# Two routed sublayers of a decoder: how scatters, sums and the hand-over to the next block are ordered

## Time and profile before

| | us |
|---|---|
| median of 3 runs | 3512.28 (3511.22 to 3514.16) |
| the profiled execution: its time | 3504.94 |
| the profiled execution: its span | 3503.2 |
| busy in the span: PE, DVE, ACT, POOL | 2806.8, 2181.1, 1821.2, 1838.3 |
| `moe_first`: to the last eviction | 463.5 |
| `moe_last`: from its first expert output to the end | 3230.1 to 3503.2 |

### The profile page before, as it was taken

The page is one execution under the profiler, slowest core; times in us unless marked ns, Lnnn a source line. Parts: engine busy times, 40 slices in busy tenths (PEclk is TensorE's granted clock), DMA queues, the critical chain, the costliest instruction groups (busy, mean ns, idle before and its releaser), DMA issues. The chain is left out here.

```text
span 3503.2 us, 84294 instructions
## 1 busy us (share of the span) xinstructions
PE 2806.8 (80%) x28622; PEld 1994.2 (57%) x28638; DVE 2181.1 (62%) x5986; ACT 1821.2 (52%) x3448; POOL 1838.3 (52%) x1742
## 2 busy tenths in 40 slices
PE   2799877978888699826469998996888679996984
PEld 2788855745555466514336665664444446665873
DVE  3022346568887588751458876776999767884124
ACT  0444447445555466502136666774567766662441
POOL 4642655347766555444655546663133755553436
PEclk9999988999999799955579999997999989996997
DMA  9565520200110221117411112221000012213653
GB/s 339 148 189 160 162 83 25 8 23 35 42 43 37 69 72 67 61 54 193 118 39 53 57 55 90 91 90 39 1 1 1 5 37 62 76 66 111 172 156 109
DMA packets 327245, 283.50 MB, mean 81 GB/s; under 512 B 111382, under 2 KB 244921, under 8 KB 326588
## 3 DMA queue, kind: packets, MB, share of 16 engines
q1 hardware_dynamic: 285324, 230.00, 22.1%
q0 software_dynamic: 16384, 33.59, 3.2%
q10 hardware_dynamic: 25264, 16.40, 1.5%
HBM read 135.30 MB, written 60.69 MB: 56 GB/s over the span
## 5 line engine op out<-in xcount | busy, mean ns | idle before, releaser
L939 DVE TENSOR_TENSOR moe_first_tile_y<-moe_first_out_ps,moe_first_expert_w 128x256 f32<-128x256 f32 x85 | 35.9, 422 | 272.1 <-PE moe_first_out_ps L1084 271.8
L797 POOL DMA_INDIRECT moe_first_token_y<-slot_y,moe_first_slots x128 | 125.0, 976 | 98.2 <-DMA slot_y<-moe_first_tile_y 59.5
L1895 POOL TENSOR_TENSOR causal_k_blocks<-causal_k_T,headmask 128x1024 f32<-128x1024 f32 x64 | 121.4, 1899 | 99.6 <-PE causal_scores L1505 94.0
L1895 POOL TENSOR_TENSOR alibi_k_blocks<-alibi_k_T,headmask 128x1024 f32<-128x1024 f32 x64 | 121.3, 1898 | 94.0 <-PE alibi_scores L1505 90.0
L1084 PEld LDWEIGHTS moe_first_out_ps<-moe_first_expert_down,moe_first_hid 128*128 128x128 f32 x1360 | 167.5, 194 | 5.4 <-issue 0.6
L1162 POOL DMA_INDIRECT slot_x<-x_tok,moe_first_slots x128 | 124.8, 975 | 85.8 <-issue 36.7
L1084 PE MATMUL moe_first_out_ps<-moe_first_expert_down,moe_first_hid 128*128 x1360 | 167.4, 277 | 0.4 <-issue 0.4
L1895 POOL TENSOR_TENSOR full_k_blocks<-full_k_T,headmask 128x1024 f32<-128x1024 f32 x64 | 120.8, 1898 | 84.9 <-PE full_scores L1505 79.9
L3188 PE MATMUL L_ffn_experts<-weights_odd,x_T 128*128 128x512 f32 x256 | 141.8, 637 | 12.3 <-ACT L_ffn_expert_out L3288 11.2
L1895 POOL TENSOR_TENSOR keys_k_blocks<-keys_k_T,headmask 128x1024 f32<-128x1024 f32 x64 | 120.9, 1900 | 45.6 <-PE keys_scores L1505 42.0
L3111 DVE SCALAR_TENSOR_TENSOR L_ffn_combined<-L_ffn_expert_out,L_ffn_mix,L_ffn_combined 128x128 f32<-128x128 f32 x448 | 138.9, 373 | 4.0
(11 more groups left out here) (580 smaller groups left out, 9044.1 us busy)
## 6 DMA issues: line engine op xcount, KB each, us to landing
moe_first_expert_w<-in_L_attn_experts SPq DMA_DIRECT2D x85, 322.0 KB
moe_last_expert_w<-in_L_ffn_experts SPq DMA_DIRECT2D x53, 322.0 KB
moe_first_tile_x<-slot_x SPq DMA_DIRECT2D x85, 128.0 KB, 2.7
slot_y<-moe_first_tile_y SPq DMA_DIRECT2D x85, 128.0 KB
slot_x<-blank ACTq DMA_DIRECT2D x2, 4992.0 KB, 43.0
L_ffn_tile_x<-slot_x SPq DMA_DIRECT2D x32, 256.0 KB, 3.2
slot_y<-L_ffn_tile_y SPq DMA_DIRECT2D x32, 256.0 KB
moe_last_tile_x<-slot_x SPq DMA_DIRECT2D x53, 128.0 KB, 2.4
```

Source lines behind the costliest of these rows:

```text
L797: pool.indirect_dma_start(y_in[:, p, k, r, :], None, slot_y[part][0:NTS[part] * SLOT_TILE, :], bass.IndirectOffsetOnAxis(slots[:, part, r, ...
L939: dve.tensor_tensor(y_out[:, q, :, :], out_bank[j % 2][:, 0:SLOT_TILE].rearrange("p (s d) -> p s d", s=SPAN), over(wall[:, j % RING, FF + ...
L1895: pool.tensor_tensor(k_blocks[:, t.p, :, :], keys.to_broadcast([128, 8, TILE]), lanes.to_broadcast([128, 8, TILE]), ALU.mult).then_inc(spr ...
```

## The change

Scatters of all parts are issued one after another with no wait on evictions, ahead of all gathers. The order on POOL is then: for each chunk, three of the next chunk's four tiles are gathered, then the inverse deviation, then the fourth. SP asks for the weights of tile j+5 ahead of the rows of tile j+8. The sums get new places (`DUE`): 37, 41, 45, 49 and 66, 69, 72, 75, 78, 81 in `moe_first`; 18, 21, 24, 27 and 41, 43, 45, 47, 49 in `moe_last`. What has no place by tile J - 4 is `held`: chunks 10 to 15 in `moe_first`, which the next block gets, and chunks 9 to 15 in `moe_last`, which follow its tile loop. Transposes and stores of a chunk come one tile later. In the block after `moe_first` a handed chunk takes two steps instead of three, with two tiles gathered in each. The gather of chunk 10 stays in `moe_first`.

```diff
--- before.py
+++ after.py
@@ -760,13 +760,14 @@
         def due(c):
 
             part = part_of[c]
-            if part == parts - 1:
-                return None
-            return reach[part + 1] + 3 + chunks[part].index(c) * (NTS[part + 1] - 4) // len(chunks[part])
-
-        after_tile = {due(c): c for c in range(CHUNKS) if due(c) is not None}
-        last_chunks = chunks[-1]
-        late = [] if hand_over else last_chunks
+            settle, apart = DUE[part]
+            return reach[part + 1] + settle + apart * chunks[part].index(c)
+
+        DUE = ((14, 4), (4, 3)) if top == 2 else ((3, 3), (3, 2))
+        FIRST = next(c for c in chunks[1] + [chunks[2][0]] if c in chunks[2] or due(c) > J - 4)
+        held = range(FIRST, CHUNKS)
+        after_tile = {due(c): c for c in range(FIRST)}
+        late = [] if hand_over else held
 
         def combine(dve, c):
             p, part = c % 2, part_of[c]
@@ -1002,13 +1003,13 @@
                 for j in range(8):
                     load_slots(j)
                 for j in range(J):
+                    if j + 5 < J:
+                        load_expert(j + 5)
                     if j + 8 < J:
                         load_slots(j + 8)
-                    if j + 5 < J:
-                        load_expert(j + 5)
                     store_slots(j)
-                    if j - 2 in after_tile:
-                        tail.store(sp, after_tile[j - 2])
+                    if j - 3 in after_tile:
+                        tail.store(sp, after_tile[j - 3])
                 for c in late:
                     tail.store(sp, c)
                 tail.all_stored(sp)
@@ -1099,8 +1100,8 @@
                     if j + 2 < J:
                         hidden(j + 2)
                     output(j)
-                    if j - 2 in after_tile:
-                        tail.transpose(pe, after_tile[j - 2], route_bank)
+                    if j - 3 in after_tile:
+                        tail.transpose(pe, after_tile[j - 3], route_bank)
                 for c in late:
                     tail.transpose(pe, c, route_bank)
 
@@ -1145,84 +1146,71 @@
                         copy_turned(j // 2 + 2)
                     if j + 2 < J:
                         activate(j + 2)
-                    if j - 2 in after_tile:
-                        tail.copy_transposed(act, after_tile[j - 2], route_bank)
+                    if j - 3 in after_tile:
+                        tail.copy_transposed(act, after_tile[j - 3], route_bank)
                 for c in late:
                     tail.copy_transposed(act, c, route_bank)
 
             @block.gpsimd
             def _(pool):
-                def scatter(part, some):
-
-                    pairs = top * sizes[part]
-                    for n in some:
+                def scatter(part):
+                    for n in range(top * sizes[part]):
                         t, r = divmod(n, top)
-                        if part and n % 2 == 0 and n:
-                            pool.wait_ge(out_done, reach[part - 1] + n * (NTS[part - 1] - 6) // pairs)
                         pool.indirect_dma_start(slot_x[part][:, :],
                                                 bass.IndirectOffsetOnAxis(slots[:, part, r, t:t + 1], 0),
                                                 net.x_tok[:, origin[part] + t, :], None).then_inc(scattered[part], 16)
-
-                def finish_chunk(c):
-                    if c == chunks[part_of[c]][0]:
-                        gather(pool, c, range(PER))
-                    if c + 1 < CHUNKS and part_of[c + 1] == part_of[c]:
-                        gather(pool, c + 1, range(PER))
-                    tail.inverse_std(pool, c)
 
                 for part in range(parts):
                     pool.wait_ge(net.cleared[part], 16)
                     net.await_rows(pool, part)
                     pool.wait_ge(planned, 2 * part + 2)
-                    pairs = top * sizes[part]
-                    if part < 2:
-                        scatter(part, range(pairs))
-                        continue
-                    turns = len(chunks[part - 2])
-                    for n, c in enumerate(chunks[part - 2]):
-                        finish_chunk(c)
-                        scatter(part, range(pairs * n // turns, pairs * (n + 1) // turns))
-                for some in chunks[max(parts - 2, 0):]:
-                    for c in some:
-                        if not hand_over or c not in last_chunks:
-                            finish_chunk(c)
+                    scatter(part)
+                gather(pool, 0, range(PER))
+                for c in range(FIRST):
+                    before = PER - 1 if part_of[c] == part_of[c + 1] else 0
+                    gather(pool, c + 1, range(before))
+                    tail.inverse_std(pool, c)
+                    gather(pool, c + 1, range(before, PER))
+                for c in late:
+                    if c + 1 < CHUNKS:
+                        gather(pool, c + 1, range(PER))
+                    tail.inverse_std(pool, c)
 
         if not hand_over:
             return
         ctx.close()
-        FIRST = last_chunks[0]
 
         def late_gpsimd(pool):
             def rows(c):
-                m, third = divmod(c, 3)
-                if m < len(last_chunks):
-                    gather(pool, FIRST + m, ((0, 1), (2,), (3,))[third])
+                m, half = divmod(c, 2)
+                if 1 <= m < len(held):
+                    gather(pool, FIRST + m, ((0, 1), (2, 3))[half])
 
             def inverse_std(c):
-                m, third = divmod(c, 3)
-                if third == 0 and m < len(last_chunks):
+                m, half = divmod(c, 2)
+                if half == 0 and m < len(held):
                     tail.inverse_std(pool, FIRST + m)
 
             return [(-5, rows), (-1, inverse_std)]
 
         def late_vector(dve):
             def weighted_sum(c):
-                m, third = divmod(c, 3)
-                if third == 0 and m < len(last_chunks):
+                m, half = divmod(c, 2)
+                if half == 0 and m < len(held):
                     combine(dve, FIRST + m)
 
             def normalise(c):
-                m, third = divmod(c, 3)
-                if third == 0 and m < len(last_chunks):
+                m, half = divmod(c, 2)
+                if half == 0 and m < len(held):
                     tail.normalise(dve, FIRST + m)
 
             return [(-2, weighted_sum), (0, normalise)]
 
         def late_tensor(pe, bank, host):
             def transpose(c):
-                m, third = divmod(c, 3)
-                if third == 0 and m < len(last_chunks):
-                    if m:
+                m, half = divmod(c, 2)
+                if half == 0 and m < len(held):
+                    if c >= 3:
                         pe.wait_ge(host.xT_copied, c - 2)
                     tail.transpose(pe, FIRST + m, bank)
 
@@ -2007,7 +1995,7 @@
 
     def copied_by(self, step):
 
-        return self.first + min(CHUNKS - self.first, max(0, (step + 2) // 3))
+        return self.first + min(CHUNKS - self.first, max(0, (step + 1) // 2))
 
 
 class Flow:
```

## The result

The changed kernel takes 3465.82 us (median of 4 runs, 3463.55 to 3468.67), the kernel before beside it 3513.22. The ratio is 0.9866, with a 95% interval from 0.9849 to 0.9883: 47 us faster, where 66 were forecast. The profiled execution took 3465.42 us with a span of 3463.7, that is 39.5 us less than the span of the profiled execution before; before's other runs lie 6 to 9 us above its profiled one, which is the difference between 39.5 and 47. The mean clock is 0.896 in both.

A forecast was written before the change was run, and what follows sets the result against it. No engine was busy throughout; PE stalls from paced scatters, and evictions held while DVE waited for gathers or deviations, were taken as the loss. Front -37.7 and end -28.4 gave -66.1: 3438.8 profiled, 3446 expected, range 3436 to 3468.

The forecast's parts named there:

- Part 1, scatters: Routed sublayers: unpaced scatters remove PE's boundary stalls, 16.51 + 1.49 + 3 and 8 us in `moe_first`, 11 and 17.5 in `moe_last`.
- the 1 us of the sum: Start of `moe_first`: price taken for DMA traffic of scatters beside the first rows and weights, bounds nothing to 7 us.
- Part 2, weights ahead of rows: SP's queue at part boundaries: weights no longer stand behind the wait for rows; counted zero, bound 1.5 us.
- Part 3, places of the sums: `moe_first`: sums spaced by the gathers' rate, 3 tiles apart, so tile 84 is evicted at 408.5 instead of 463.1.
- The terms -54.6 and +1: `moe_first`: saving of 54.6 us to the last eviction, and 1 us lost to DMA traffic at the start.
- Part 4, the hand-over: Block after `moe_first`: six handed chunks, two overlapping steps each, rounds of 21 us; 2.3 us less ahead, price 16.8.
- The term of 16.8: Block after `moe_first`: price in us of handing over six chunks, 112.2 to attention chunk 10's moments where before 95.4.
- The rivals of a round of 26.9 or 38 us: Hand-over rounds stay as long as three-step ones (+25 us, 3471, chance 0.10), or steps don't overlap (3536, chance 0.03).
- DVE shutting POOL out: Block after `moe_first`: rival that six handed sums and normalisations each stop POOL, +20 us, 3466, chance 0.04.
- The front's sum, -37.7: First sublayer and the block after it, in us: -54.6 + 1.4 + 1 - 2.3 + 16.8.
- the 2.3 of the rounds: Block after `moe_first`: 12 gathers instead of 14 ahead of the first handed deviation, 16.5 us instead of 18.8.
- Part 5, the end: Last sublayer: without stalls and with closer sums, the last gather starts at 3457.9 instead of 3486.34, saving 28.4 us.

## Why the prediction was right, and which of its steps were not

**Part 1, scatters.** Right on the chips of the kind that the profile before came from, step by step: scatters every 1.265 us to 192.5, no wait of PE at a boundary in either sublayer. The start was 0.6 us later (first eviction 94.91 instead of 94.34), within the 1 us of the sum. That the trace of one chip doesn't show what scatters do to PE elsewhere was not among the rivals. That both stalls went because the pacing did is read from the timelines: no run on such a chip took the pacing alone away or put it back.

**Part 2, weights ahead of rows.** Counted as nothing; no run changes it alone, so this is neither shown nor refuted.

**Part 3, places of the sums.** Last eviction 407.8 against 408.5 and the later start. DVE's waits for the gathers' sums are gone, and what is left is 10 waits for the deviation, 13.4 us together, while PE waits 0.2 us in the whole loop. The terms -54.6 and +1 measured as 407.8 - 463.1 = -55.3.

**Part 4, the hand-over.** Two steps a chunk overlap as argued. The term of 16.8 measured as 114.5 - 95.4 = 19.1: the first round took 23.3, and DVE's next sum stands ahead of the first normalisation there (that this is the cause was not tested). The rivals of a round of 26.9 or 38 us fall. The price of the first was worked out wrongly, too: three rounds of 26.9 instead of 21 cost 17.7 us and not 25. DVE shutting POOL out falls as well: the gathers beside the handed sum at 417.0 took 0.95 to 1.00 us. The 1.16 us of the earlier trace rows is not shown to be DVE's doing: that gather is the first behind other work of POOL, and the one at 326.99, the first behind a wait, took 1.09 with DVE idle.

**The step that was missing: the end of the sublayer.** The forecast lets the block begin 1.6 us after the last eviction, as before, and adds 1.4 for chunk 9's transposes. It began 9.1 after it. POOL now works until the end, and its drain, which had ended together with SP's work, lies open: 9.1 - 3.0 = 6.1 us. The front's sum, -37.7, measured as 548.7 - 580.3 = -31.6 us at attention chunk 10. The 6.1 missing are the drain; the 2.3 of the rounds are made up by the earlier last eviction (1.7) and a first handed deviation that ends 17.3 us after the block's start instead of 17.9 (20.2 less 2.3).

**The step that failed: "took the rest as unchanged".** The instructions of diff and what follows are unchanged, their time is not. Moved forward by 32.6 us, they take 23.0 us more in all (32.6 - 9.6), of which 18.6 are in diff, where PE's clock falls again and again. The runs with a delay of 0.6 and 1.2 us showed that shifting diff against the clock's fall is enough to change this; for the 4.4 behind diff nothing was tested. By the profiles: forecast 66.1, less 6.1 at the front, plus 1.0 between attention chunk 10 and L_ffn's end, plus 1.5 in the last sublayer (29.9 for 28.4), less 23.0: the measured 39.5. Before's other executions are slower than its profiled one, so by the medians the loss is smaller: 66.1 less 6.1, plus 2.5, less the measured 47.4 leaves 15.1 us for it.

The Trainium skill, TensorE: Matmul & The Clock Gate (section "Part 1: The HAM clock gate"), says that the chip judges PE's activity in windows that run on by themselves and don't start anew with the kernel, so that the moment of the turn varies from run to run, and puts the penalty of the first ramp under 1% of a typical span. The traces agree that the position decides, but not that it varies: the fall ahead of diff lies at the same place in four executions of three kernels, on at least two chips, and after's pattern came back the same in its repeat. The loss here, of later falls and not of the first ramp, is 0.7% of the span by the profiles, but a third of the forecast gain (23 of 66 us).

**Part 5, the end.** Right: 28.4 us at the gathers of chunk 4, 29.9 at the last deviation, 26 to 27 in the run that changed it alone.

## What to carry to other kernels

A stage that becomes shorter moves all that follows, and an unchanged stage with short pauses of PE may then run at another clock. Before believing or giving up a change of some 10 us, shift the stage behind it by a microsecond and see whether the time jumps. If an engine ends a stage with indirect DMAs, look for its drain: to stay hidden here it needed POOL's last work 5 to 9 us before the other engines were done. And try a long unbroken stream of POOL's indirect DMAs on more than one chip: the change with it saved 47 us on one kind of chip, and on another three kernels with it were 69 to 75 us slower than before, so pacing that looks like waste may be a guard.

## What the runs showed of the hardware

- The sets of runs are of two kinds: the kernel before took 3513 to 3515 us in three of them, 3650 and 3630 in two, each of these on a chip of its own. Whether it is the chip or its condition at the time isn't shown. In the slower ones PE's issue dropped, to as little as one matmul in 2.8 us at a DMA share of 0.16, while POOL issued indirect DMAs back to back; in one place it began 10 us after they did. The cause isn't shown.
- POOL's drain at the end of the two routed sublayers' blocks took 5.8 to 11.0 us as recorded in every kernel here, 9.0 us in the one other block with indirect DMAs where it was read, and 0.3 to 1.1 us in five blocks without. Part of the record can lie beside POOL's last work. It also sets the end of the whole kernel: after, DVE's last work starts at 3453.4 and SP is through at 3456.9, but POOL's drain runs from 3452.3 to 3462.6. The Trainium skill, VectorE: DVE Perf Modes (section "The DRAIN you can't avoid"), knows, beside the drain behind each DVE instruction, one on all five engines ahead of and behind the kernel, a constant of about 12 ns. SP's is 7 to 137 ns here; POOL's is not of that kind.
- The clock's falls are bound to the work and not to chance: ahead of diff it fell 2.6 us before the start in four executions without a delay, 3.2 and 3.8 us with delays of 0.6 and 1.2 us (an estimate from the windows' means). The kernel with 1.2 us more pause there was some 14 us faster, 3450.86 against 3464.74 us, on another chip.
